# A graph network on one core: scatters that add, a comparison within one tile, and four sets of blocks instead of three

## What is computed

```python
h = relu(layernorm(x))                                  # before each of the four
# L0: a weight for each edge, from a small network on both of its ends
ew = sigmoid(gelu(concat(h[src], h[dst]) @ mlp_w1 + mlp_b1) @ mlp_w2 + mlp_b2)
norm = dinv[src] * ew * dinv[dst]                       # dinv = 1/sqrt(sum of ew at a node)
x = x + segment_sum((h @ conv_w)[src] * norm, dst) + conv_b
# L1: twice relu(gcn(h)); L2: a message and an update network; L3: three gcn
def gcn(h): return segment_sum((h @ W)[src] * dis[src] * dis[dst], dst) + b   # dis = 1/sqrt(degree)
agg = segment_sum(m[senders], receivers)                # L2, m from a two-layer network
```

## Time and profile before

| | us |
|---|---|
| runs shown | 5878.09, 5878.37, 5882.56 |
| their median | 5878.37 |
| the profiled execution | 5869.91 |
| its span | 5868.2 |

### The profile page before, as it was taken

The page is one execution under the profiler, slowest core; times in us unless marked ns, Lnnn a source line. Parts: engine busy times, 40 slices in busy tenths (PEclk is TensorE's granted clock), DMA queues, the critical chain, the costliest instruction groups (busy, mean ns, idle before and its releaser), DMA issues.

```text
span 5868.2 us, 82106 instructions
## 1 busy us (share of the span) xinstructions
PE 3758.9 (64%) x26427; PEld 2570.5 (44%) x26427; DVE 2498.4 (43%) x11277; ACT 1229.7 (21%) x3130; POOL 1736.7 (30%) x1749
## 2 busy tenths in 40 slices
PE   3444444444000000007667999999999999999999
PEld 2333333333000000006555666666666666666666
DVE  6666766676101000009997222454344333333111
ACT  2454444444000000005554000111111000000000
POOL 4665666666777777760000000000000000000000
PEclk7555555555555555559998999999999999999999
DMA  5777777776100000007772565455555566566665
GB/s 151 233 228 232 230 232 224 232 231 207 22 1 23 11 7 11 11 8 231 238 236 98 177 193 181 160 164 176 160 165 167 170 191 192 181 190 191 187 199 170
DMA packets 456936, 925.35 MB, mean 158 GB/s; under 512 B 81052, under 2 KB 318060, under 8 KB 449868
## 3 DMA queue, kind: packets, MB, share of 16 engines
q1 hardware_dynamic: 382668, 830.57, 44.1%
q0 software_dynamic: 69312, 87.75, 6.2%
q10 hardware_dynamic: 4544, 1.77, 0.1%
HBM read 739.99 MB, written 179.87 MB: 157 GB/s over the span
## 4 chain that ended last, share of the span: by engine, by line
PE 46%; another core or an unknown queue 24%; DVE 16%; issue 8%; ACT 3%; DVEq 1%; DMA 0%; SPq 0%; ACTq 0%
PE ps L1030 40%; DVE same L1296 3%; DVE inv_all L1399 3%; PE ps L1064 1%; ACT apart L746 1%; DVE onehot_b L1327 1%; DVEq L478 1%; PE ps L1073 1%; DVE scaled L1339 1%; DVE acc L1413 1%; DVE h L1413 1%; ACT apart L749 1%; PE ps L1040 1%; DVE pre L1335 1%
## 5 line engine op out<-in xcount | busy, mean ns | idle before, releaser
L1030 PE MATMUL ps<-parts,halves 128*128 128x384 bf16 x14553 | 2476.2, 326 | 6.1 <-DVE parts L1470 5.6
L1030 PEld LDWEIGHTS ps<-parts,halves 128*128 128x128 f16 x14553 | 1425.4, 98 | 887.8 <-DVE parts L1470 7.1
L660 POOL DMA_INDIRECT rows<-table,src_of x880 | 842.7, 958 | 583.9 <-DVE pre L1335 299.9
L668 POOL DMA_INDIRECT adj<-count,place x832 | 869.1, 1045 | 270.5 <-issue 270.5
L1499 DVE TENSOR_REDUCE summed_f<-ps 128x128 f32<-128x384 f32 x277 | 154.5, 558 | 1394.8 <-PE ps L1040 1307.7
L940 PE MATMUL ps<-dst_mlp,onehot_t 128*128 x2640 | 364.5, 232 | 562.0 <-issue 329.5
L963 PE MATMUL ps<-inv_parts,low_t 128*128 128x49 bf16 x2640 | 130.7, 189 | 673.3 <-issue 523.9
L940 PEld LDWEIGHTS ps<-dst_mlp,onehot_t 128*128 128x128 bf16 x2640 | 275.8, 104 | 640.7 <-issue 583.9
L1399 DVE SCALAR_TENSOR_TENSOR inv_all<-chunk_iota,chunk_of,ps 128x49 f32<-128x49 f32 x880 | 181.9, 263 | 798.9 <-remote 796.8
L771 ACT ACTIVATE onehot<-plain,norm 128x128 f32<-128x128 bf16 x880 | 281.0, 390 | 1016.5 <-issue 754.3
L1296 DVE SCALAR_TENSOR_TENSOR same<-spare_sum,key,ps 128x128 bf16<-128x128 f32 (+2 forms) x832 | 488.1, 588 | 6.5 <-DMA spare_sum<-key_list 6.3
(11 more groups left out here) (255 smaller groups left out, 3586.7 us busy)
## 6 DMA issues: line engine op xcount, KB each, us to landing
halves<-adj SPq DMA_DIRECT2D x297, 800.0 KB, 4.5
halves<-adj SPq DMA_DIRECT2D x297, 768.0 KB, 4.4
adj<-slot_of SPq DMA_DIRECT2D x52, 1568.0 KB
h_rows<-rows SPq DMA_DIRECT2D x220, 256.0 KB
rows<-h_rows SPq DMA_DIRECT2D x220, 256.0 KB
spare_sum<-key_list SPq DMA_DIRECT2D x104, 512.0 KB
onehot_list<-onehot_b SPq DMA_DIRECT2D x220, 128.0 KB
low_row<-low_list SPq DMA_DIRECT2D x220, 128.0 KB
```

The source lines that it names most:

```text
L660: nc.gpsimd.indirect_dma_start(out=rows_0[:, g % RING, s, :], out_offset=None, in_=table[:, :], in_offset=bass.IndirectOffsetOnAxis(ap=src ...
L668: nc.gpsimd.indirect_dma_start(out=adj[:, :], out_offset=bass.IndirectOffsetOnAxis(ap=place[:, k:k + 1], axis=0), in_=count16[:, k:k + 1], ...
L1030: last = nc.tensor.matmul(ps_sum[u % 3], halves[:, n % AR, c - at, :], parts[q % 2][:, c, :, :].rearrange("p t d -> p (t d)"), start=(c == ...
```

## The change

The diff, cut to its core; `...` marks what is left out:

```diff
-SETS = ((0, 26), (26, 41), (41, 49))
+SETS = ((0, 26), (26, 36), (36, 45), (45, 49))
...
-EARLY = [[(0, 24, 0, 25)], [], []]
+EARLY = [[(0, 26, 0, 25)], [(26, 36, 0, 25), (0, 36, 25, 35)], [(36, 45, 0, 35)], []]
...
         def load_keys(eng, n):
             after(eng, compared, RUN_TILES * (n - KEYS + 1))
-            after(eng, crossed, (RUN_TILES - CROSS) * (n - KEYS + 1))
...
                     nc.gpsimd.indirect_dma_start(out=adj[:, :], out_offset=bass.IndirectOffsetOnAxis(ap=place[:, k:k + 1], axis=0),
-                                                 in_=count16[:, k:k + 1], in_offset=None).then_inc(scattered[s], 16)
+                                                 in_=count16[:, k:k + 1], in_offset=None, compute_op=ALU.add).then_inc(scattered[s], 16)
...
-            def compare_earlier(g):
...
-            act.wait_ge(cross_clear, 1)
-            pipeline(GROUPS, [(1, copy_onehot), (3, tanh_group), (2, gelu_group), (0, clear_sums), (0, compare_earlier)])
+            pipeline(GROUPS, [(1, copy_onehot), (3, tanh_group), (2, gelu_group), (0, clear_sums)])
...
-                r0 = 0 if r < CROSS else r
                 after(dve, compared, t - 1)
-                nc.vector.scalar_tensor_tensor(same[r % 2][:, 0:r + 1 - r0, :], key_row[:, n % KEYS, r0:r + 1, :], key[:, t:t + 1],
-                                               ps_weight[:, CROSS - 1 - r + r0:CROSS, :], ALU.is_equal, ALU.mult,
+                nc.vector.scalar_tensor_tensor(same[r % 2][:, 0:1, :], key_row[:, n % KEYS, r:r + 1, :], key[:, t:t + 1],
+                                               ps_weight[:, CROSS - 1:CROSS, :], ALU.is_equal, ALU.mult,
                                                accum_out=count[:, batch % 2, r * S + i:r * S + i + 1]).then_inc(compared, 1)
...
                 dve.wait_ge(compared, BATCH * (b + 1))
-                dve.wait_ge(crossed, (RUN_TILES - CROSS) * S * (b + 1))
-                nc.vector.tensor_tensor(of, of, cross[:, b % 2], ALU.add).then_inc(deduping, 1)
```

25 lines of the change are left out of this document (2 added, 23 removed).

## The result

| | before | after |
|---|---|---|
| median of 4 runs | 5878.23 us | 5116.07 us (5112.15 to 5123.76) |
| span of the profiled execution | 5868.2 us | 5115.6 us |
| ratio | | 0.8705, interval 0.8695 to 0.8716 |

The changed kernel is 13% faster. That is 762 us where 78 were forecast. It lies inside the range, between the two sums of rival 1 (4725 and 5333 us).

The account below looks back on a forecast made before the run. First loop, scatters, second loop and layers were taken to stand one behind another, other engines crawling beside the scatters. 5868.2 - 130 + 0 + 8 + 44 = 5790, with 10 more 5800 us; range 4700 to 6500.

Parts of the forecast that it names:

- rival 1: Scatters: adding ones leave other engines free, so the second loop runs beside them; 4725 us, or 5333 at 2.32 us each; chance 0.28.
- Part 1: First loop: smaller comparisons on DVE and none on ACT save 0.6 us a group, 130 us, between 50 and 280.
- Rival 3: First loop gets no faster, as unexplained waits fill the time the comparison leaves; gain 0 to 50, 5880 to 5930 us; chance 0.08.
- Part 2: Scatters: an add costs what a copy does, 1.37 us each, so 0 us, between -20 and +790; other engines' crawl stays.
- The crawl: Beside the scatters, PE runs one instruction each 1.40 us and a second-loop group takes 55.99 us, not 2.20; taken as unchanged.
- rival 2: Scatters: an adding one takes POOL longer, half a gather's price (+395 us, 6195) or the whole (6590 us); chance 0.27.
- Parts 3 and 4: Layers: four sets cost one more spare unit, +8 us; more early sums make 45 late blocks 4.56 us each, +44 us.
- part 3: Layer 0: four sets add one spare unit, +8 us; no wait of SP or PE for scatters there.

Follow-up runs that it names:

- e2: Changed kernel with copying scatters instead of adding ones: 4576.57 us, beside 4554.24 us for the kernel before.
- e14: Changed kernel with copying scatters and a POOL memset of 448 numbers a partition ahead of each: 4959.13 us, beside 5874.01 us for the kernel before.
- e15: Changed kernel with copying scatters of only the first 64 of 128 elements, half the edges left out: 5916.46 us, beside 5874.01 us for the kernel before.
- e8: Changed kernel with the three sets and 24 early sums of before, adding scatters kept: 5262.53 us, 115.3 us more than the changed kernel.
- e1: Kernel before with one edit, its scatters add, comparisons with earlier tiles kept: 4992.41 us, beside 4554.24 us for the kernel before.
- e5: Changed kernel unchanged, run again beside the kernel before: 5147.20 us against 5909.34 us, ratio 0.8706.
- e16: Changed kernel with each run's first tile copied, 160 scatters moved into the first loop, clears ahead of them: 5074.77 us, ratio 0.8644 to the kernel before.

## Why the prediction was wrong

**Part 1, wrong in size.** Forecast -130 us between -50 and -280; measured -15 (last gather 1473.9 to 1459.1). The step that failed is "together 16.1% of 6.29 us is 1.0 us a group". It took a share of the chain as time that comes back. The stops of all engines were there in the earlier trace rows as 46.9%, and the arithmetic stood in their shadow: DVE's share fell and theirs rose. Rival 3 was right on this part, that the waits "stay and fill the time that the comparison leaves". The floor of 5.0 us a group was right for the first kind (5.04 us in e2).

**Part 2, both steps wrong.** The price of the add: forecast 0 within -0.02 and +0.95 us; measured 1.56 instead of 0.97 us on POOL and 1.90 instead of 1.37 us between two, +0.53. "Issue time follows the number of elements and not what is done with them" fell: the rows were both copies and could not show it. It is a little more than the half of a gather's price that rival 2 had (0.47 us). The Trainium skill (DMA: Bandwidth & Descriptors, section "SDMA does more than copy") describes the add as a reduction of two streams, from which the prediction drew a time on this side; the trace has one. The crawl: "I also take the crawl of the other engines as it is". It was held by "element count, 2-byte size and pace stay". The pace did not stay, and a slower pace is enough: e14 has the element count, size and kind of write of before, and the crawl is gone. Beside its pace only the other parts of the change are new in it, and with those e15 still crawls.

The two steps belong together. I had a dearer add under rival 2 and a freed second loop under rival 1, as if they were independent, with the first a loss. It was the dearer issue that freed the second loop. Rival 1 had the stage right and the reason wrong, since it hung the crawl on what a transfer does. That the add's price came out above the pace of the crawl was foreseen by neither, and the gain is luck as far as the prediction goes. Rival 1's own sum with the measured values, 1460 + 832 x 1.90 = 3041, plus 44 + 2004 + 10, is 5099 us, 17 below the median. Its 44 us behind the last scatter were 71, in which PE did not wait for it. From my sum of 5790 us to the span of 5116 it is +115 (part 1), +440 (the add), -1066 (second loop and layer 0 no longer behind the scatters) and -163 (the moved chunks now leave the path: -111 instead of +52), together -674.

The numbers that point to it stood ahead of the prediction. POOL issued each 1.37 us, PE moved each 1.40 us, and the crawl outlasted the last scatter by 27 us. 832 x (1.40 - 1.37) is 25 us. A tail of that length after 832 issues fits a backlog that never emptied, so that a slightly slower issue would empty it. That reading was made with e14 and e15 in hand.

**Parts 3 and 4, right.** Late blocks of layer 1: forecast 4.56 us with PE idle before the turn. PE's timeline of one, against the earlier trace rows:

```profile
3199.71 0.33 PE L1016 MATMUL ps<-spare_parts,slot_of 128*128 128x384 bf16 x1
...
3203.04 0.30 PE L1029 MATMUL ps<-ident,source 128*128 128x128 f32 x1 [0.86 <-DVE source L1467]
...
3204.28 0.33 PE L1016 MATMUL ps<-spare_parts,slot_of 128*128 128x384 bf16 x1
```

4.57 us, 3.33 to the turn, 0.86 idle. What follows layer 0 was put at 2004 us and takes 2007. In part 3 the 569 us of layer 0 hold three spare units (49 x 9.13 + 3 x 8.0 + 97.5) and not two, as its words say; the sum is right. "No wait of SP or PE for scatters in layer 0" was wrong, as a consequence of part 2, and with it "the four sets pay only here" came true: 115 us (e8).

**The chances.** Forecast 0.37, rival 1 0.28. The range held the time because it was 1800 us wide. Rival 1's time should have had more weight by the tail of 27 us, as I read it now. The condition that I did not see is outside the kernel: on chips of the first kind an adding scatter loses 438 us (e1).

## What to carry to other kernels

When an engine slows down to about one instruction for each DMA that another issues, compare the pace of issue with that of the others and look how long the crawl lasts after the last issue. If the tail is the count times the difference, a backlog is the first thing to test, and a slightly slower issue, by a pause or dearer instruction, may be worth more than a faster one. A share of a chain whose largest item is unexplained waits is no estimate of what comes back when a small item is removed. And a gain that rests on such a stall should be measured on more than one chip, since it can turn around where the stall is absent.

## What the runs showed of the hardware

- Two kinds of visits with the same kernel, on six chips: 4554 to 4560 us on four, 5874 and 5909 us on two. The layers run alike, at a granted clock of 1.00 (2.4 GHz). The windows of e2 on the first kind and of e15 on the second:

```profile
3500.00:4000.00 500.00, 500.00 (x3135) 313.61 (x3134) 159.55 (x527) 15.44 (x58) 0.00 (x0) 1.00 0.60 187
```
```profile
4800.00:5300.00 500.00, 500.00 (x3135) 313.65 (x3133) 159.61 (x527) 15.38 (x58) 0.00 (x0) 1.00 0.60 188
```

  The DMA engines work as long too. The page's queues of e2:

```profile
q1 hardware_dynamic: 389580, 833.79, 57.5%
q0 software_dynamic: 69312, 87.75, 7.7%
```

and of e15, which has the same packets:

```profile
q1 hardware_dynamic: 389580, 833.79, 44.0%
q0 software_dynamic: 69312, 87.64, 6.0%
```

  0.575 x 4574.8 = 2631 us against 0.440 x 5914.7 = 2602 us, 0.077 x 4574.8 = 352 us against 355 us. So what takes 1.40 us for each scatter is not the moving of its packets.
- What it is stays open. It is not scatters that have not landed: each waits for the landing of the one four before, while the tail of 25 to 27 us is the time of 18 or 19 of them. That PE gets through one instruction at a time, in step with the scatters, speaks against a late supply of instructions in blocks, of which the page counts 230 and 176 packets for 5.2 MB, 13 KB each; that DVE and ACT run their part of a group in one go does not. The Trainium skill (NOTIFIC — the notification-queue block, section "The write path") says of the block that writes the engines' trace records that its internal pipeline holds producers back rather than lose a record. No run here shows whether that is at work.
- An adding scatter of 128 elements of 2 bytes costs POOL 1.56 us, a copying one 0.97 us, a copying one of 64 elements 0.90 us. The add has 112 more packets for each scatter, 144 against 32.
- On the second kind a POOL transfer in the first loop takes 1.59 us in the mean with gathers alone (e5, 440 in 700 us) and 1.51 us with one in five a scatter (e16, 332 in 500 us); on the first kind 1.26 us (e2, 556 in 700 us).
